# One transformer block on one core: third stage with its query halves first, its mask in four small products, and the last sum and store tile by tile

## The reference, cut to what matters

```python
x = x + self_attention(layernorm(x))          # 16 heads of 8
x = x + cross_attention(layernorm(x), ctx)    # 16 heads of 64
x = x + local(layernorm(x))                   # DEPTH = 6 layers, below
# one layer of local(y):
s = shift_tokens(y)                           # second half of the columns moved down one row
q, k, v = split(s @ Wqkv)                     # 16 heads of 64
q, k = l2norm(q) * qs, l2norm(k) * ks         # then rotary, with tables for q and for k
p = softmax(where(mask, -max, 8 * q @ k.T))   # mask: key after query, or over 32 rows before it
y = p @ v @ Wo + y
h = layernorm(shift_tokens(y)) * g + b
a, gate = split(h @ W1 + b1)                  # 341 columns each
y = a * gelu(gate) @ W2 + b2 + y
# the output is x + y after the sixth layer
```

## Time and profile before

| | us |
|---|---|
| median of 3 runs (3785.45 to 3789.49) | 3785.52 |
| the profiled execution's own time | 3781.1 |
| its span, first to last instruction | 3779.3 |
| busy: PE / DVE / ACT / POOL | 3614.2 / 2785.0 / 2905.5 / 2588.6 |

### The profile page before, as it was taken

The page is one execution under the profiler, slowest core; times in us unless marked ns, Lnnn a source line. Parts: engine busy times, 40 slices in busy tenths (PEclk is TensorE's granted clock), DMA queues, the critical chain, the costliest instruction groups (busy, mean ns, idle before and its releaser), DMA issues. The chain is left out here.

```text
span 3779.3 us, 124845 instructions
## 1 busy us (share of the span) xinstructions
PE 3614.2 (96%) x50565; PEld 2635.3 (70%) x50757; DVE 2785.0 (74%) x5266; ACT 2905.5 (77%) x5539; POOL 2588.6 (68%) x4812
## 2 busy tenths in 40 slices
PE   6989997999999999999999999999999999999996
PEld 4778874677677777776777767777667777777765
DVE  5834446788777877777777777778777787777874
ACT  4756664788888888888888888888888888888885
POOL 4622225777777777777777777777777777777773
PEclk9999999999999999999999999999999999999998
DMA  3000000000000000000000000000000000000001
GB/s 94 3 10 9 8 5 19 17 10 10 10 19 21 18 10 10 10 23 24 10 10 10 15 25 18 10 9 10 24 24 10 9 10 16 14 10 9 10 10 28
DMA packets 145046, 59.08 MB, mean 16 GB/s; under 512 B 116954, under 2 KB 139231, under 8 KB 144479
## 3 DMA queue, kind: packets, MB, share of 16 engines
q1 hardware_dynamic: 144478, 51.08, 5.5%
HBM read 23.95 MB, written 2.10 MB: 7 GB/s over the span
## 5 line engine op out<-in xcount | busy, mean ns | idle before, releaser
L1341 DVE TENSOR_TENSOR R<-bank,tables 128x1024 f32<-128x1024 f32 x768 | 919.5, 1218 | 243.0 <-ACT sq L1247 242.7
L1043 PE MATMUL bank<-WA,xcT 128*128 128x512 f32 x1536 | 694.5, 595 | 4.6 <-ACT xcT L1221 2.7
L1247 ACT ACTIVATE sq<-bank 128x512 f32<-128x512 f32 x768 | 459.3, 598 | 159.9 <-PE bank L1043 159.9
L1446 POOL TENSOR_TENSOR R<-R 128x512 f32<-128x512 f32 x384 | 481.1, 1275 | 0.0
L1043 PEld LDWEIGHTS bank<-WA,xcT 128*128 128x128 f32 x1536 | 277.2, 190 | 284.1 <-issue 190.8
L1221 ACT ACTIVATE qT<-bank 128x512 f32<-128x512 f32 x384 | 229.7, 598 | 286.9 <-PE bank L1125 286.9
L1356 DVE TENSOR_REDUCE ss<-sq 128x16 f32<-128x1024 f32 x384 | 444.3, 1198 | 4.4 <-ACT sq L1247 4.2
L1095 PE MATMUL bank<-WV,xcT 128*64 128x512 f32 x1536 | 414.2, 618 | 0.0
L1460 POOL TENSOR_TENSOR P<-P,rn 128x512 f32<-128x512 f32 x384 | 404.9, 1055 | 0.6 <-DVE P L1384 0.6
L1466 POOL TENSOR_TENSOR P<-P,inv_sum 128x512 f32<-128x512 f32 x384 | 403.1, 1050 | 0.8 <-DVE inv_sum L1396 0.8
L1187 PE MATMUL bank<-WO,OT 128*128 128x128 f32 x3072 | 396.8, 283 | 0.0
(11 more groups left out here) (157 smaller groups left out, 7818.2 us busy)
## 6 DMA issues: line engine op xcount, KB each, us to landing
WA<-in_wqkv SPq DMA_DIRECT2D x24, 256.0 KB, 2.9
ystat<-Y SPq DMA_DIRECT2D x192, 32.0 KB
ystat<-Y SPq DMA_DIRECT2D x384, 15.8 KB
ys<-Y SPq DMA_DIRECT2D x192, 32.0 KB
ys<-Y SPq DMA_DIRECT2D x384, 15.8 KB
WV<-in_wqkv SPq DMA_DIRECT2D x6, 512.0 KB, 3.7
WO<-in_wo SPq DMA_DIRECT2D x6, 512.0 KB, 4.4
X<-in_x SPq DMA_DIRECT2D x4, 512.0 KB, 5.1
```

What stands on the lines that cost most here:

```text
L1043: mm(b[QK_BANK[n, half]][:, :], m.xsT[:, k % 2, :], cols[:, half, :, :], start=True, stop=True)\
L1247: nc.scalar.activation(by_half[:, half, :, :], b[QK_BANK[n, half]][:, :].rearrange("p (h d) -> p h d", d=32), ACT.Square)\
L1341: tt(both, src.unsqueeze(1).to_broadcast([128, 2, 16, 32]), tab.unsqueeze(2).to_broadcast([128, 2, 16, 32]), ALU.mult).then_inc(s.rotated, 1)
L1446: tt(m.R[:, KEYS, 0, at], m.R[:, KEYS, 0, at], m.R[:, KEYS, 1, at], ALU.add).then_inc(s.k_added, 1)
```

## The change

Three edits, all in or behind the third stage.

1. The halves stand in the order queries 0, queries 1, keys 1, keys 0, on PE, ACT and DVE. DVE's rotary of queries 1 moves up to right behind that of queries 0, the sum of the queries' squares follows it, then the statistics, then the sum of the keys' squares. The keys' products still wait for the feed-forward sum (s.y); queries 1 no longer stands behind that wait.
2. The mask is written by four products of a 64x64 identity with the 64-row mask pattern, one for each quadrant, in the same round as the scores.
3. finish is gone. In the last layer DVE adds each tile's Y to its X right behind ff_added, and SP stores 256 KB for every four tiles, one turn later.

```diff
@@ queries_keys (PE)
                     heads_in(t, k, QUERIES, 0)
+                    if filling(t, 7):
+                        at_least(pe, s.q_copied, 2 * t - 1)
+                    heads_in(t, k, QUERIES, 1)
                     at_least(pe, s.y, t - 6)
                     if filling(t, 7):
                         at_least(pe, s.rotated, 4 * t)
                     heads_in(t, k, KEYS, 1)
-                    if filling(t, 7):
-                        at_least(pe, s.q_copied, 2 * t - 1)
-                    heads_in(t, k, QUERIES, 1)
                     heads_in(t, k, KEYS, 0)
@@ scores (PE)
-                    for a in range(2):
-                        mm(S_BANK[a][:, :], m.identb[:, :], m.causalb[:, :], start=True, stop=False)
+                    crossed = ((0, 0), (1, 1), (0, 1), (1, 0))
+                    for a, bb in crossed:
+                        half = slice(64 * a, 64 * a + 64)
+                        mm(S_BANK[a][64 * bb:64 * bb + 64, :], m.identb[half, half], m.causalb[half, :],
+                           start=True, stop=False)
@@ turn (ACT)
                 squares(i, QUERIES, 0, 0)
-                squares(i, KEYS, 1, 1)
-                squares(i, QUERIES, 1, 2)
+                squares(i, QUERIES, 1, 1)
+                squares(i, KEYS, 1, 2)
                 squares(i, KEYS, 0, 3)
@@ ff_added (DVE)
                     tt(y, y, FF_OUT[:, 0:128], ALU.add).then_inc(s.y, 1)
+                    if layer(t) == DEPTH - 1:
+                        x = tile_of(m.X, t)
+                        dve.wait_ge(s.y, t + 1)
+                        tt(x, x, y, ALU.add).then_inc(s.final, 1)
@@ turn (DVE)
                 rotary(i, QUERIES, 0, 1)
+                rotary(i, QUERIES, 1, 2)
+                squares_summed(i, k, QUERIES)
                 statistics(i - 5, k - 5)
-                squares_summed(i, k, QUERIES)
                 squares_summed(i, k, KEYS)
-                rotary(i, QUERIES, 1, 3)
                 seeded(i, k)
@@ local (SP)
+            def store(n):
+                if n > 0 and n % STORED == 0:
+                    part = slice(n - STORED, n)
+                    sp.wait_ge(s.final, n)
+                    sp.dma_start(out[:, part, :], m.X[:, part, :]).then_inc(s.stored, 16)
             def turn(i, k, l):
                 layer_input(i + 1, k + 1, l)
                 ff_input(i - 5, k - 5)
+                store(i - LAST - (N - TILES))
```

More of the change, by code:

```diff
@@ L178, in build @@
         local(nc, sem, m)
-        finish(nc, sem, m)
 def setup(nc, sem, m):
@@ L267, in _ @@
             act.activation(m.wqk[:, :], m.bank[1][:, 0:128], ACT.Copy)
[L270 to L290, removed]
 def load_input_weights(sp, m, l, par, c):
@@ L889 @@
 QUERIES, KEYS = 0, 1
+STORED = 4
 FIRST, LAST = 0, 7
@@ L943, in local @@
     s.ff, s.gelu, s.h, s.w2, s.y = sem("local_ff"), sem("local_gelu"), sem("local_h"), sem("local_w2"), sem("local_y")
+    s.final, s.stored = sem("local_final"), sem("local_stored")
     held = sem("local_held")
@@ L950, in layer @@
         return t // TILES
+    out = m.out.rearrange("(t b) s d -> (b s) t d", b=2)
     with nc.Block() as block:
@@ L1007, in _ @@
                     load_value_weights(sp, m, l + 1)
-            for i in range(N, N + 5):
+            for i in range(N, N + LAST + 1):
                 turn(i, i % 2, DEPTH)
+            sp.wait_ge(s.stored, 16 * (TILES // STORED))
         @block.tensor
@@ L1102, in scores @@
                     pe.wait_ge(s.k_copied, 2 * t + 2)
-                    for a in range(2):
-                        mm(S_BANK[a][:, :], m.identb[:, :], m.causalb[:, :], start=True, stop=False)
+                    crossed = ((0, 0), (1, 1), (0, 1), (1, 0))
[3 more added lines that the diff above has]
+                           start=True, stop=False)
                     for hp in range(PAIRS):
-                        for a, bb in ((0, 0), (1, 1), (0, 1), (1, 0)):
+                        for a, bb in crossed:
                             head, at = slice(64 * a, 64 * a + 64), hp * 128 + bb * 64
@@ L1243, in squares @@
                     act.wait_ge(s.qk, 4 * t + at + 1)
-                    if at < 2:
+                    if at % 2 == 0:
                         at_least(act, s.summed, 2 * t - 1 + n)
@@ L1354, in squares_summed @@
                 if inside(t, N):
-                    dve.wait_ge(s.squared, 4 * t + 3 + n)
+                    dve.wait_ge(s.squared, 4 * t + 2 + 2 * n)
                     nc.vector.tensor_reduce(m.ss[:, k % 2, 16 * n:16 * n + 16],
```

## The result

| | us |
|---|---|
| before, median of 4 | 3786.34 |
| after, median of 4 (3678.14 to 3680.48) | 3679.71 |
| ratio, 95% interval | 0.9716, 0.970 to 0.9733 |
| span of the profiled execution, before and after | 3779.3, 3678.6 |

The change saves 106.6 us. The forecast was 90, and 3679.7 lies 4 us under the lower end of the range (3684).

What follows compares the result with a forecast made beforehand. PE was taken to bound the kernel, with a path through ACT and DVE nearly as long. Savings 56.1 + 5.6 + 18 + 2.5 + 6.9 = 89.1 us from 3781.1 gave 3692, stated as 3696 with 4.4 for the median; 8-in-10 range 3684 to 3735.

Steps and rivals of the forecast that it cites:

- the two paths: Inside a turn: PE's own work, about 16.18 us, and PE to ACT's squares to DVE to PE, 16.21.
- the regular turn: Third stage: each of 187 turns falls from 16.21 to 15.88 us, 0.33 less.
- What bounds the kernel: Third stage: PE is busy 16.05 of 16.21 us a turn and waits briefly for DVE's second rotary pass.
- The wait for R: PE's query transposes wait 0.03 us a turn for DVE's second rotary pass; removing it saves 5.6 us.
- The mask: PE's mask block, first weight load to first score: from 0.54 to 0.24 us, saving 0.30 a turn, 56.1 us.
- Late DMAs: DVE's statistics wait for late DMAs and delay the rotary pass; 18 of 20 us in long turns saved.
- What is late next: After the change: POOL's chain, ACT's normalisation, then its copy of the transposed queries fit with 0.15 us of room.
- Filling, sum and store: First turns save 2.5 us; last-layer sums cost nothing, and the end after the last sum saves 6.9 us.
- Pairs: Rival: only two of four mask products run at once, block 0.45 us, 37 us back, 3734; chance 0.12.
- one after the other: Rival: the four mask products run serially, block 0.87 us, turn 16.51, 3814, slower; chance 0.05.
- DVE's chain: Rival: DVE's work still sets the turn, so the mask change gives nothing, 3752; chance 0.04.
- the late part: Rival: statistics, normalisation and copies become the path, or long turns have another cause; 3714 or 3733; chance 0.13.

Runs made afterwards that it cites:

- e1_halves: Kernel before with only the new order of the halves and of DVE's turn, old mask and finish: 3753.97 us against 3785.68, ratio 0.9915.
- e2_mask: Kernel before with only the mask in four small products, old order and finish: 3784.21 us, ratio 0.9996.
- e5_mask_twice: Changed kernel with the round of four mask products issued twice, the second adding to the first: 3716.46 us, turns of 16.024.
- e9_stats_early: Changed kernel with DVE's statistics moved back between the two rotary passes of the queries: 3689.35 us, ratio 0.9743.
- e3_stats_late: Kernel before with only DVE's statistics call moved behind the second rotary pass of the queries: 3793.40 us, ratio 1.002.
- e10_mask_rows: Changed kernel with the four mask products ordered so that two of one row half follow one another: 3679.88 us, turns of 15.811.
- e7_mask_tall: Changed kernel with the mask in two products of 64 by 128 instead of four of 64 by 64: 3705.75 us, ratio 0.9792.
- e6_no_mask: Changed kernel with the mask left out, each score issued with start=True: 3647.13 us, turns of 15.63.

## Why the prediction was wrong

The direction, the two paths and the order of the terms were right, and one term, the regular turn, was too small. The sum came out 16 us short: 12.7 in the regular turns, 1.7 in the long ones, 0.5 in the filling and 1.1 in draining and end.

- *What bounds the kernel.* Right: two paths of nearly one length (e1_halves, e2_mask). The wait for R was 0.04 a turn and not 0.03; I had read it from one turn.
- *The mask.* The block was right to 0.01 us, and so was that all four run at once (e5_mask_twice). **The step that failed is where this term ended: at the first score.** I took the scores' stretch as 1.09 on either side and gave its change no term. With a mask of their own shape ahead, their loads start early and the stretch is 1.03. Mask and wait for R, 61.7 us in the sum (0.33 x 187), measured 74.4 (0.398 x 187): 0.061 x 187 = 11 us of the difference are the loads, and 1 to 2 the wait for R. The upper bound of 0.33 for the mask's saving left this out too, and so the range's lower end was too high.
- *Late DMAs.* Right in kind, 19.7 and not 18. Two things did it: R moved ahead of the statistics, and the statistics went late. The first alone leaves 8.3 us of long turns (e9_stats_early).
- *What is late next.* Right: the chain to ACT has 0.14 of room left where I said 0.15, and the copies of the queries are no later than before. e3_stats_late shows the price when PE does have to wait for them. The next limit on DVE's side, the passes that empty banks for PE (e9_stats_early), is not in the prediction.
- *Filling, sum and store.* The filling gave 3.0 for 2.5, draining and end 0.3 and 7.7 for 6.9. The stores of 256 KB landed in 2.4 us (median), where I had 3.0: from the last store's issue to the span's end it is 2.7 us.
- *Rivals.* Pairs and one after the other are excluded by e5_mask_twice, DVE's chain and the late part by the profile after.

## What to carry to other kernels

Price a block on TensorE to the end of the block behind it, since what stands ahead can decide whether that block's loads run early (1.03 or 1.09 us for the same 64 products). Where two paths have nearly one length, shorten both: here the order alone gave 32 us, the mask alone nothing and both together 98. And a call that is moved to relieve one engine is to be followed through every in-order queue behind it: the same move of the statistics lost 8 us or gained 27, depending on the place of one call on ACT.

## What was not expected of the hardware

- Four 64x64 quadrants take bf16 streams of 512 columns at once: 0.213 us for four more of them, and the same turn with two products of one row half behind one another (e10_mask_rows).
- A change of shape ahead of the scores costs about 0.08 us as an edge, and 0.06 more because the loads that follow it do not run ahead. The 0.06 were seen behind three other shapes: 128x128 (e1_halves), 64x128 (e7_mask_tall) and 128x64 (e6_no_mask). The 0.08 rest on e7_mask_tall alone, which has two products where the change has four; nothing here separates shape from number.
- The small DMAs of the statistics land late now and then: in the kernel before, DVE waited for them in 36 turns between 1000 and 3600 us, by up to 1.5 us. Why they do is open.
